# A selective scan with its decays in a ring of three buffers instead of two, the third in SBUF

## The chip, the cores and the metric

The kernel runs on one core of one Trainium2 chip. The metric is the device time of one execution in microseconds (us). The kernel before took 1248.2 us in the median of three runs (1247.94 to 1252.96). The profiler recorded one further execution.

Five engines work side by side, each through its own list of instructions: TensorE (PE; its weight loads are listed as PEld), VectorE (DVE), ScalarE (ACT), GpSimd (POOL) and SyncE (SP), which here issues the DMAs. They wait for each other by semaphores.

## The reference, cut to what matters

Four layers follow each other over 2048 tokens of 128 channels: a state-space mixer, causal attention with a mixture of eight experts, a second state-space mixer, and a gated feed-forward net. The change is in the second mixer, whose core is a linear recurrence over time, one for each of 256 channels and 16 states:

```python
delta = softplus(delta_s @ dt_proj_w + dt_proj_b)
A = -jnp.arange(1, d_state + 1)                    # d_state = 16
deltaA = jnp.exp(delta[..., None] * A)             # the decays
deltaB_u = delta[..., None] * B[:, :, None, :] * u[..., None]
def step(h, inp):
    dA, dBu_ = inp
    h = dA * h + dBu_
    return (h, h.sum(-1))                          # the sum over the 16 states
y = y + u * D
y = y * silu(z)
return y @ out_proj_w + out_proj_b
```

## The kernel before, in words

The scan stage works through NB = 4 blocks of 512 tokens, and in each through NS1 = 16 states, so 64 steps that the program numbers k = 16 b + n. The 256 channels lie as two halves (j = 0, 1) on 128 partitions. For each step:

- **ACT** writes the decays exp(-(n+1) delta) of both halves, 128 x 1024 numbers, into `decay[k % 2]` (`state_act`, L2096). The two buffers are four PSUM banks. From k = 2 on it first waits until step k - 2 has been scanned.
- **POOL** writes the drives delta u B into `drive[k % 5]` (`state_pool`, L2142), 128 x 1024 numbers. It reads `du` and a broadcast row of B, both in SBUF, and writes SBUF.
- **DVE** runs two scans of 512 tokens (`state_dve`, L2164), one for each half. Each reads its decays from PSUM and its drives from SBUF, starts from the last state of the block before (`hlast`, one number for each partition), and writes `hst[k % 4]` in SBUF.
- **PE** adds `hst` into two PSUM banks by matmuls with the identity (`state_sum_pe`, L2083), three steps behind.
- **ACT** copies the last column of `hst` into `hlast` (`state_last_act`, L2171). In its list this stands right behind the decays of step k and is for step k - 2.

DVE waits at step k for the decays and drives of k, for the sum of step k - 4 and for the copy of step k - 4, since `hst` has four buffers. POOL waits for the scan of step k - 5, since `drive` has five.

Between the steps other work is placed by tables written out by hand, each entry a step n within the block and a part: `FRONT_ACT`, `FRONT_DVE`, `FRONT_PE` and `FRONT_POOL` prepare the next block (input projection, convolution, activations, delta, u, B), `POST_*` finish the block before, `FW_ACT` and `FW_POOL` split the weights of the following net into a high and a low part (L2441 on ACT, `lo_part` L675 on POOL), and `NET_*` begin that net. On ACT the order within a step is: decays, copy of a last state, front parts, weights. Front parts that matter below are "z" and "tap" at n = 3 (L2009, L2002), "xc" and "gate" at n = 7 (L2016, L2019, in another activation table), "db" at n = 8, "dt" at n = 11 (L2040, another table again) and "u" at n = 12. On DVE "conv0" and "conv1" stand at n = 4 and 5 (L2064), "du" at n = 13 (L2075), the output of the block before (`scan_y_dve`, L2178 and L2182) ahead of step n = 3.

Before the first step the experts finish. Their last additions on DVE are L1709 (`acc`, both inputs in SBUF), their low parts on DVE are L675 (`hx_lo`, both inputs in SBUF). The low weights of the last expert lie in `ew_lo3` at offset A_END, a region of 6144 bytes of each partition that nothing uses once `down_done` is complete.

Of the kernel before, what the change touches and what calls it, by code (L numbers as in the profile page):

```python
# [5 lines left out]
F32 = mybir.dt.float32  # L6
# [3 lines left out]
ACT = mybir.ActivationFunctionType  # L10
AX = mybir.AxisListType

P = 128
T = 2048
D = 128
BLK = 512
# [16 lines left out]
NS1 = 16  # L33
HBUF = 4
DRIVE_SLOTS = 5
# [61 lines left out]
def build(nc, a):  # L97
# [10 lines left out]
    def sb(name, shape, dt, at=None):  # L108
        size = 4 if dt in (F32, F32R) else 2
        for s in shape[1:]:  # L110
            size *= s
        size = (size + 31) // 32 * 32
        if at is None:
            at = free[0]
            free[0] += size
        t = nc.alloc_sbuf_tensor_at(name, shape, dt, offset=at + BASE)
        t_end[name] = at + size
        return t

    t_end = {}  # L120
    BASE = (nc.sbuf_base + 31) // 32 * 32
    with ctx:
# [82 lines left out]
        A_END = free[0]  # L205
# [11 lines left out]
        W_END = A_END + 6144  # L217
# [100 lines left out]
        delta = sb("delta", [P, 2, 2, BLK], F32)  # L318
# [3 lines left out]
        drive = sb("drive", [P, DRIVE_SLOTS, 2, BLK], F32)  # L322
        assert t_end["drive"] - 4096 <= t_end["hid"]
        b_bc.append(sb("b_bc1", [P, B_ROWS, BLK], F32))
        hst = sb("hst", [P, HBUF, 2, BLK], F32)
# [3 lines left out]
        fh = sb("fh", [P, HC, BLK], F32)  # L329
        fo = sb("fo", [P, 2, BLK], F32)  # L330
        assert free[0] <= W_END, (free[0], W_END)
        free[0] = t_end["sz1_even"]
        fh_first = [sb("fh_hi0", [P, HC, BLK], F32R), sb("fh_lo0", [P, HC, BLK], F32R)]
        fa = sb("fa", [P, 2, BLK], F32)
# [8 lines left out]
        psum = ctx.enter_context(nc.psum_tensor("psum", [P, 8, BLK], F32))  # L343
# [791 lines left out]
        def route_at(table, k, step):  # L1135

            return table.get(LAST_STEPS * (k - 14) + step) if k >= 14 else None
# [7 lines left out]
        for k in range(16):  # L1145
            for step in range(2 * (ITEMS[k][0] + 1)):
# [8 lines left out]
                if route_at(ROUTE_PE, k, step):  # L1155
                    kind, b = route_at(ROUTE_PE, k, step)
                    plan(("route_" + kind, b))
                if (k, step) in PREP_PE:
                    b, part = PREP_PE[k, step]
# [345 lines left out]
        N_UNITS = len(UNITS)  # L1505
# [392 lines left out]
        NET_STATS, NET_LN, NET_APPLY, NET_TURN, NET_HI = 7, 9, (11, 12), 13, 14  # L1898
        b_rows = nc.dram_tensor("b_rows", (NB, NS1, BLK), F32, kind="Internal").ap()
        B_FROM = 16 * (NE // RAW_SLOTS)  # L1900
        decay = [psum[:, 4:6, :], psum[:, 2:4, :]]

        def front_parts(table, k):

            return [((k - at) // NS1 + 1, part) for at, part in table
                    if (k - at) % NS1 == 0 and 1 <= (k - at) // NS1 + 1 < NB]
# [14 lines left out]
        for k in range(NB * NS1):  # L1921
            b, n = divmod(k, NS1)
# [163 lines left out]
        def state_act(act, b, n):  # L2086
            k = NS1 * b + n
            if n == 0:
                act.wait_ge(S["c_dt_read"], 2 * b + 2)
            if k == 0:  # L2090
                act.wait_ge(S["gelu_done"], FC * N_UNITS)
            if k == 1:
                act.wait_ge(S["y_gated"], N_UNITS)
            if k >= 2:
                act.wait_ge(S["scanned"], k - 1)
            act.activation(decay[k % 2], delta[:, b % 2, :, :], ACT.Exp, scale=-float(n + 1)).then_inc(S["decay_done"], 1)  # L2096

        def b_save_sp(sp, b):
            sp.wait_ge(S["c_db_read"], b + 1)
# [55 lines left out]
        def state_dve(o, dve, b, n):  # L2155
            k = NS1 * b + n
            dve.wait_ge(S["decay_done"], k + 1)
            dve.wait_ge(S["drive_done"], k + 1)
            if k >= HBUF:
                dve.wait_ge(S["summed"], k - HBUF + 1)  # L2160
                dve.wait_ge(S["hlast_done"], k - HBUF + 1)
            for j in range(2):
                init = 0.0 if b == 0 else hlast[:, n, j:j + 1]
                ins = dve.tensor_tensor_scan(hst[:, k % HBUF, j, :], decay[k % 2][:, j, :], drive[:, k % DRIVE_SLOTS, j, :], init,  # L2164
                                             ALU.mult, ALU.add)
            ins.then_inc(S["scanned"], 1)

        def state_last_act(act, b, n):
            k = NS1 * b + n
            act.wait_ge(S["scanned"], k + 1)  # L2170
            act.activation(hlast[:, n, :], hst[:, k % HBUF, :, BLK - 1], ACT.Copy).then_inc(S["hlast_done"], 1)  # L2171
# [44 lines left out]
        def scan_act(o, act):  # L2216
            for b in range(NB):
                for n in range(NS1):
                    state_act(act, b, n)
                    if NS1 * b + n >= 2:  # L2220
                        state_last_act(act, *divmod(NS1 * b + n - 2, NS1))
                    for nb, part in front_parts(FRONT_ACT, NS1 * b + n):
                        scan_front_act(o, act, nb, part)
                    if n in FW_ACT and 3 * b + FW_ACT[n] < 11:
                        fweights_act(act, 3 * b + FW_ACT[n])
                    if b == NB - 1 and n in NET_APPLY:
                        net_apply_act(act, NET_APPLY.index(n))
                    if (b, n) == (NB - 1, NET_HI):
                        net_hi_act(act, 0)

        def scan_dve(o, dve):
            for b in range(NB):
                for n in range(NS1):
                    if n == POST_Y and b >= 1:
                        scan_y_dve(o, dve, b - 1)
                    state_dve(o, dve, b, n)
                    if b == 0 and n == 0:
                        experts_add_dve(dve, NB - 1)
                    if n == POST_DVE and b >= 1:
                        scan_post_dve(dve, b - 1)  # L2240
                    if (b, n) == (NB - 1, NET_STATS):
                        net_stats_dve(o, dve)
                    for nb, part in front_parts(FRONT_DVE, NS1 * b + n):
                        scan_front_dve(o, dve, nb, part)
            net_lo_dve(dve, 0)
            scan_y_dve(o, dve, NB - 1)
# [94 lines left out]
        def net_apply_act(act, half):  # L2341
            if half == 0:
                act.wait_ge(S["ln_rstd"], LN_D + 1)
                act.wait_ge(S["ln_turned"], LN_D)
            for i in range(TPB // 2 * half, TPB // 2 * (half + 1)):
                ins = act.activation(xn[:, i, :], x_tok[:, i, :], ACT.Identity, scale=ln_rs[:, 0, i:i + 1], bias=ln_nb[:, i:i + 1])
            if half == 1:
                ins.then_inc(S["ln_xn"], 1)

        def net_hi_act(act, b):  # L2350
            act.wait_ge(S["ln_turned"], LN_D + b + 1)
            act.activation(xT[0][:, :], net_x(b)[:, :], ACT.Copy).then_inc(S["xT_hi"], 1)
# [86 lines left out]
        def fweights_act(act, c):  # L2439
            act.wait_ge(fw_in[c % 2], 16 * (c // 2 + 1))  # L2440
            act.activation(fw_hi[:, 4 * c:4 * c + 4, :], fw_raw[:, c % 2, :, :], ACT.Copy).then_inc(S["fw_hi"], 1)  # L2441
# [95 lines left out]
        @block.scalar  # L2537
        def _(act):
            o = Order(act, S["act_order"])
            act.wait_ge(S["in_x"], 32)  # L2540
            act.activation(half_gate[:, :], cols[:, COL["b_gate"]:COL["b_gate"] + 2], ACT.Copy, scale=0.5)
            act.activation(a_neg[:, :], C("a_log"), ACT.Exp).then_inc(S["a_ready"], 1)
            for n in range(5):
                front_act(o, act, 0, n)
            for g in range(G_END):
                if g < G:
                    chunk_act(act, g)
                for what, b, n in mixer_parts(g):
                    if what == "front":
                        front_act(o, act, b, n)  # L2550
                    elif what == "prep":
                        for part in PREP_STEP_ACT[n]:
                            prep_act(act, b, part)
                    else:
                        end_act(act, b, n)
            early_act(act, "f")
            act.wait_ge(S["x_mixed"], NB)
            attention_act(act)
            moe_act(o, act)
            scan_act(o, act)  # L2560
            net_act(act)
# [173 lines left out]
```

## Time and profile before

| | |
|---|---|
| median of 3 runs | 1248.2 us |
| the profiled execution's own time | 1252.22 us |
| its span, first to last instruction | 1249.9 us |
| busy over the span | PE 90%, DVE 75%, ACT 63%, PEld 48%, POOL 26% |
| mean granted TensorE clock | 0.969 of full speed |
| scan stage | from about 910 to about 1110 us of the span |

A row of a timeline names when an instruction or a run of like instructions began, how long it took, the engine, the line of the kernel, what was written and read with shapes, how many there were, and in brackets how long the engine had been idle before it and what released it. Like instructions that follow each other are merged into one row (x2, x10). Durations of neighbours on one engine overlap by some hundredths of a us.

### The profile page before, as it was taken

Reading aid. Unit: us, or ns where it says so; the run is one execution under the profiler, and the core shown is the slowest. Engines: PE = TensorE matmul, PEld = TensorE weight load, DVE = VectorE, ACT = ScalarE, POOL = GpSimd, SP = SyncE. Lnnn points to the kernel's source line nnn. Section 1 sums busy time; section 2 is a strip of 40 time slices with the busy share of each in tenths; the row PEclk is TensorE's granted clock in tenths of the full one; section 3 lists DMA queues with packets and bytes.
Section 4 is the critical chain, followed back from the end, with each engine's and each line's share of the span. In section 5 each row is a group of like instructions: output and inputs, shape, how many; then the busy total and the mean of one; then the engine's idle time right before and its main releaser. Section 6 shows DMA issues by size and latency. Waiting matters only on the chain.

```text
span 1249.9 us, 16003 instructions
## 1 busy us (share of the span) xinstructions
PE 1120.0 (90%) x5702; PEld 594.1 (48%) x5702; DVE 931.8 (75%) x1737; ACT 783.9 (63%) x1156; POOL 327.6 (26%) x271
## 2 busy tenths in 40 slices
PE   5889878888999999989999899999979789799998
PEld 2455554443333333333322288887633334357776
DVE  4788678857887888878864188887789999984432
ACT  4767632455655656656678898667758677455554
POOL 4233332210000000000012131210179788840000
PEclk9789889999998999999999999999989999899999
DMA  5211464345000000000000132211223222200000
GB/s 152 79 41 69 122 148 102 86 102 119 2 1 1 2 1 2 1 1 1 2 19 12 42 109 66 78 51 36 84 84 111 85 110 93 102 1 6 4 9 18
DMA packets 30623, 67.29 MB, mean 54 GB/s; under 512 B 3952, under 2 KB 16240, under 8 KB 28496
## 3 DMA queue, kind: packets, MB, share of 16 engines
q1 hardware_dynamic: 30544, 66.27, 18.5%
q8 instruction: 46, 0.75, 0.3%
q14 instruction: 33, 0.27, 0.1%
HBM read 57.47 MB, written 8.78 MB: 53 GB/s over the span
## 4 chain that ended last, share of the span: by engine, by line
PE 57%; DVE 14%; POOL 9%; issue 8%; ACT 7%; DMA 1%; SPq 0%; DVEq 0%; POOLq 0%; ACTq 0%
PE psum L1353 8%; PE psum L1238 8%; PE psum L405 7%; PE psum L407 7%; PE psum L406 7%; PE psum L1307 7%; POOL drive L2142 6%; DVE mx L1250 6%; DVE hst L2164 2%; ACT probs L1321 2%; PE psum L551 1%; PE psum L543 1%; PE psum L475 1%; PE psum L1956 1%; DMA m_rows<-mrow 1%
## 5 line engine op out<-in xcount | busy, mean ns | idle before, releaser
L1250 DVE TENSOR_REDUCE mx<-psum 128x1 f32<-128x512 f32 (+3 forms) x640 | 349.2, 603 | 64.8 <-PE psum L1238 35.2
L1321 ACT ACTIVATE probs<-psum 128x1024 f32<-128x1024 f32 (+1 forms) x320 | 283.6, 936 | 173.7 <-PE psum L1307 152.7
L1238 PE MATMUL psum<-kz,qa 128*128 128x512 bf16 (+3 forms) x640 | 199.3, 354 | 18.5 <-DVE mx L1250 12.8
L1307 PE MATMUL psum<-qa,kz 128*128 128x512 bf16 (+1 forms) x640 | 176.2, 363 | 7.8 <-DMA qa<-m_rows 4.4
L2142 POOL TENSOR_TENSOR drive<-du,b_bc 128x1024 f32<-128x1024 f32 x64 | 149.5, 2367 | 10.6 <-DVE hx_lo L675 9.1
L1353 PE MATMUL psum<-probs,v 128*32 128x512 f32 (+3 forms) x1280 | 150.8, 541 | 1.5 <-POOL probs L1332 1.4
L1238 PEld LDWEIGHTS psum<-kz,qa 128*128 128x128 bf16 x640 | 57.2, 97 | 180.5 <-DVE mx L1250 131.9
L2083 PE MATMUL psum<-hst,ident 128*128 128x512 f32 x256 | 120.3, 614 | 22.7 <-DVE u L2182 14.1
L1332 POOL TENSOR_SCALAR_AFFINE_SELECT probs<-probs 128x512 f32<-128x512 f32 x48 | 29.4, 637 | 361.1 <-ACT probs L1321 361.1
L2164 DVE TENSOR_TENSOR_SCAN hst<-psum,hlast,drive 128x512 f32<-128x512 f32 x96 | 115.2, 1261 | 8.7 <-ACT psum L2096 5.0
L675 DVE TENSOR_TENSOR hx_lo<-hid,hx_hi 128x1024 fp32r<-128x1024 f32 x64 | 81.4, 1276 | 33.9 <-ACT hx_hi L1679 29.8
L2096 ACT ACTIVATE psum<-delta 128x1024 f32<-128x1024 f32 x64 | 65.6, 1026 | 51.5 <-DVE hst L2164 51.4
L1673 ACT ACTIVATE hid<-psum,cols 128x512 f32<-128x512 f32 x128 | 81.5, 681 | 21.2 <-PE psum L407 21.0
L2083 PEld LDWEIGHTS psum<-hst,ident 128*128 128x128 f32 x256 | 48.4, 196 | 88.7 <-issue 68.1
L1307 PEld LDWEIGHTS psum<-qa,kz 128*128 128x128 bf16 x640 | 57.6, 99 | 68.1 <-ACT probs L1321 27.3
L675 DVE TENSOR_TENSOR fh_lo<-fh,fh_hi 128x512 fp32r<-128x512 f32 x48 | 32.1, 688 | 57.7 <-ACT fh_hi L2371 57.7
L405 PE MATMUL psum<-fh_hi,fw_lo 128*128 128x512 f32 x144 | 57.9, 402 | 3.6 <-DVE fh_lo L675 3.6
L407 PE MATMUL psum<-fh_hi,fw_hi 128*128 128x512 f32 x144 | 56.9, 395 | 0.0
L406 PE MATMUL psum<-fh_lo,fw_hi 128*128 128x512 f32 x144 | 56.7, 394 | 0.0
L1241 PE MATMUL psum<-identb,maskneg 128*128 128x128 bf16 x256 | 55.5, 221 | 0.0
L405 PE MATMUL psum<-nx_hi,ew_lo 128*128 128x512 f32 x128 | 52.5, 411 | 3.2 <-ACT hid L1673 2.2
L2370 ACT ACTIVATE fh<-psum,cols 128x512 f32<-128x512 f32 x32 | 22.1, 689 | 48.9 <-PE psum L407 48.9
(294 smaller groups left out, 1944.6 us busy)
## 6 DMA issues: line engine op xcount, KB each, us to landing
b_bc<-b_rows SPq DMA_DIRECT2D x16, 1024.0 KB, 4.7
cs_bc<-cs_rows SPq DMA_DIRECT2D x16, 512.0 KB, 4.8
gate_bc<-gate_rows SPq DMA_DIRECT2D x32, 256.0 KB, 3.1
qk_part_rows<-qk_parts SPq DMA_DIRECT2D x48, 128.0 KB, 2.3
ew_raw<-experts_dram SPq DMA_DIRECT2D x8, 512.0 KB, 3.6
qa<-qk_part_rows SPq DMA_DIRECT2D x16, 192.0 KB, 5.3
kz<-qk_part_rows SPq DMA_DIRECT2D x16, 192.0 KB, 5.8
fw_raw<-net_dram SPq DMA_DIRECT2D x11, 256.0 KB, 2.7
```

Source lines behind the costliest of these rows:

```text
L405: pe.matmul(out, w[1], x[0], start=start, stop=False, skip_group_check=True)
L406: pe.matmul(out, w[0], x[1], start=False, stop=False, skip_group_check=True)
L407: return pe.matmul(out, w[0], x[0], start=False, stop=stop, skip_group_check=True)
L675: return dve.tensor_tensor(out, value, hi.bitcast(F32), ALU.subtract)
L1238: ins = pe.matmul(out[:, 0:w], qa[:, b, h // 2, i * P:(i + 1) * P], key_rows(h, c)[:, 0:w], start=True, stop=not last, skip_group_check=True)
L1250: dve.tensor_reduce(mx[:, 4 * i + h % 4, c:c + 1], fill_bank("mx", k, n)[:, 0:w], AX.X, ALU.max).then_inc(S["mx_read"], 1)
L1307: ins = pe.matmul(out[:, lo:], key_rows(h, kt // TPB)[:, kt % TPB * P:(kt % TPB + 1) * P], qa[:, b, h // 2, lo:], start=True, stop=not dia ...
L1321: act.activation(probs[:, st % 2, hh, :, lo:], s_pair[n % 2][:, :, lo:], ACT.Exp, scale=SCALE).then_inc(S["p_done"], 1)
L1353: ins = pe.matmul(out[32 * hh:32 * hh + 32, own:], v9[:, at:at + 32], probs[:, st % 2, hh, j, own:], start=(kt == 0), stop=(kt == TPB * (b ...
L2083: ins = pe.matmul(bank[j][:, :], ident[:, :], hst[:, (NS1 * b + n) % HBUF, j, :], start=(n == 0), stop=(n == NS1 - 1))
L2142: pool.tensor_tensor(drive[:, k % DRIVE_SLOTS, :, :], du[:, b % 2, :, :], rows.unsqueeze(1).broadcast_to([P, 2, BLK]), ALU.mult).then_inc( ...
L2164: ins = dve.tensor_tensor_scan(hst[:, k % HBUF, j, :], decay[k % 2][:, j, :], drive[:, k % DRIVE_SLOTS, j, :], init, ALU.mult, ALU.add)
```

## The change

The ring of decays gets a third buffer, `decay_sb`, 128 x 1024 floats in SBUF where `ew_lo3` lay. Step k uses buffer k % 3: steps 2, 5, 8, ... 62 (21 of 64) have their decays in SBUF, the others in PSUM as before. ACT waits for the scan of step k - 3 instead of k - 2 before it writes, and once, at k = 2, until the last expert's matmuls are done. The copy of the last state that stands behind the decays of step k is for step k - 3 instead of k - 2.

```diff
@@ -329,6 +329,8 @@
         assert free[0] <= W_END, (free[0], W_END)
+        decay_sb = sb("decay_sb", [P, 2, BLK], F32, at=A_END)
+        assert t_end["decay_sb"] <= W_END
         free[0] = t_end["sz1_even"]
@@ -1898,7 +1900,8 @@
-        decay = [psum[:, 4:6, :], psum[:, 2:4, :]]
+        decay = [psum[:, 4:6, :], psum[:, 2:4, :], decay_sb[:, :, :]]
+        ND = len(decay)
@@ -2091,9 +2094,11 @@
                 act.wait_ge(S["y_gated"], N_UNITS)
-            if k >= 2:
-                act.wait_ge(S["scanned"], k - 1)
-            act.activation(decay[k % 2], delta[:, b % 2, :, :], ACT.Exp, scale=-float(n + 1)).then_inc(S["decay_done"], 1)
+            if k == 2:
+                act.wait_ge(S["down_done"], N_UNITS)
+            if k >= ND:
+                act.wait_ge(S["scanned"], k - ND + 1)
+            act.activation(decay[k % ND], delta[:, b % 2, :, :], ACT.Exp, scale=-float(n + 1)).then_inc(S["decay_done"], 1)
@@ -2161,7 +2166,7 @@
-                ins = dve.tensor_tensor_scan(hst[:, k % HBUF, j, :], decay[k % 2][:, j, :], drive[:, k % DRIVE_SLOTS, j, :], init,
+                ins = dve.tensor_tensor_scan(hst[:, k % HBUF, j, :], decay[k % ND][:, j, :], drive[:, k % DRIVE_SLOTS, j, :], init,
@@ -2217,8 +2222,8 @@
                     state_act(act, b, n)
-                    if NS1 * b + n >= 2:
-                        state_last_act(act, *divmod(NS1 * b + n - 2, NS1))
+                    if NS1 * b + n >= ND:
+                        state_last_act(act, *divmod(NS1 * b + n - ND, NS1))
```

## Rows read from the trace of the kernel before

**Rows 1.** Scan stage: us, then busy of PE, PEld, DVE, ACT, POOL, clock, DMA share, GB/s

```profile
909.90:1109.80 199.90, 162.93 (x400) 70.77 (x398) 184.83 (x197) 128.72 (x212) 171.55 (x90) 0.95 0.26 91
```

**Rows 2.** What DVE waited for in the scan stage: total us, times, longest

```profile
DVE hst L2164 <- ACT psum L2096: 11.0, 7, 2.8
```

**Rows 3.** Timeline of DVE: scans that began late because of ACT's decays

```profile
921.18 6.89 DVE L2164 TENSOR_TENSOR_SCAN hst<-psum,drive 128x512 f32<-128x512 f32 x6 [2.76 <-ACT psum L2096]
...
954.53 4.82 DVE L2164 TENSOR_TENSOR_SCAN hst<-psum,drive 128x512 f32<-128x512 f32 x4 [1.68 <-ACT psum L2096]
...
978.13 2.46 DVE L2164 TENSOR_TENSOR_SCAN hst<-psum,hlast,drive 128x512 f32<-128x512 f32 x2 [1.10 <-ACT psum L2096]
...
1043.14 2.46 DVE L2164 TENSOR_TENSOR_SCAN hst<-psum,hlast,drive 128x512 f32<-128x512 f32 x2 [1.07 <-ACT psum L2096]
...
1054.68 4.94 DVE L2164 TENSOR_TENSOR_SCAN hst<-psum,hlast,drive 128x512 f32<-128x512 f32 x4 [1.44 <-ACT psum L2096]
```

**Rows 4.** Timeline of ACT ahead of the late scans of 954.53 and 978.13

```profile
948.42 1.03 ACT L2096 ACTIVATE psum<-delta 128x1024 f32<-128x1024 f32 x1 [1.08 <-DVE hst L2164]
...
949.60 1.28 ACT L2040 ACT_TABLE_LOAD   x1
...
974.70 1.27 ACT L2009 ACTIVATE sz_even<-psum,cols 128x512 f32<-128x512 f32 x2 [3.61 <-DVE u L2182]
```

**Rows 5.** Scan stage, groups on POOL, then DVE's scans: busy us, mean ns, idle before

```profile
L2142 POOL TENSOR_TENSOR drive<-du,b_bc 128x1024 f32<-128x1024 f32 x64 | 149.5, 2367 | 10.6 <-DVE hx_lo L675 9.1 <-issue 1.4
L675 POOL TENSOR_TENSOR fw_lo<-fw_raw,fw_hi 128x512 fp32r<-128x512 f32 x11 | 14.0, 1274 | 14.7 <-ACT fw_hi L2441 14.7
L2251 POOL TENSOR_TENSOR x_tok<-x_tok,out_b 128x512 f32<-128x512 f32 x3 | 3.8, 1267 | 6.1 <-DVE x_tok L2198 6.1
...
L2164 DVE TENSOR_TENSOR_SCAN hst<-psum,hlast,drive 128x512 f32<-128x512 f32 x96 | 115.2, 1261 | 8.7 <-ACT psum L2096 5.0 <-PE psum L2083 3.3 <-issue 0.3
```

**Rows 6.** Lines L1709 and L2142 by themselves: ns min/median/max

```profile
L1709 DVE TENSOR_TENSOR acc<-acc,y_gate x28: 661/692/2408, 745.3 to 913.5; 128x512 f32<-128x512 f32 x28
...
L2142 POOL TENSOR_TENSOR drive<-du,b_bc x64: 2338/2354/2789, 909.9 to 1104.8; 128x1024 f32<-128x1024 f32 x64
```

**Rows 7.** Timeline of POOL, then of DVE, where the drives meet DVE's last additions

```profile
909.92 2.38 POOL L2142 TENSOR_TENSOR drive<-du,b_bc 128x1024 f32<-128x1024 f32 x1 [9.15 <-DVE hx_lo L675]
...
912.26 2.79 POOL L2142 TENSOR_TENSOR drive<-du,b_bc 128x1024 f32<-128x1024 f32 x1
...
915.01 2.79 POOL L2142 TENSOR_TENSOR drive<-du,b_bc 128x1024 f32<-128x1024 f32 x1
...
910.44 2.41 DVE L1709 TENSOR_TENSOR acc<-acc,y_gate 128x512 f32<-128x512 f32 x1
...
915.52 2.32 DVE L2164 TENSOR_TENSOR_SCAN hst<-psum,drive 128x512 f32<-128x512 f32 x2
```

**Rows 8.** Timeline around 730 us, DVE and POOL by turns

```profile
730.42 1.22 DVE L675 TENSOR_TENSOR hx_lo<-hid,hx_hi 128x1024 fp32r<-128x1024 f32 x1
...
730.90 1.89 POOL L1856 TENSOR_TENSOR x_tok<-x_tok,inner 128x512 f32<-128x512 f32 x1
...
731.55 2.33 DVE L675 TENSOR_TENSOR hx_lo<-hid,hx_hi 128x1024 fp32r<-128x1024 f32 x1
...
732.75 2.27 POOL L675 TENSOR_TENSOR ew_lo<-ew_raw,ew_hi 128x512 fp32r<-128x512 f32 x1
```

**Rows 9.** Merged runs of drives and scans at the stage's end

```profile
1095.51 11.62 POOL L2142 TENSOR_TENSOR drive<-du,b_bc 128x1024 f32<-128x1024 f32 x5
...
1097.95 11.86 DVE L2164 TENSOR_TENSOR_SCAN hst<-psum,hlast,drive 128x512 f32<-128x512 f32 x10 [0.35 <-issue]
```

**Rows 10.** PE's sums at the full and at the lower clock, and the scan behind them

```profile
926.49 8.75 PE L2083 MATMUL psum<-hst,ident 128*128 128x512 f32 x20
...
1075.33 3.76 PE psum L2083 x4
...
1079.28 9.51 DVE L2164 TENSOR_TENSOR_SCAN hst<-psum,hlast,drive 128x512 f32<-128x512 f32 x8 [1.74 <-PE psum L2083]
```

## The prediction

> **What bounds the kernel now.** I read first the busy times of the stretch that the change touches [rows 1]: the scan stage lasts about 200 us, and DVE is busy for 184.8 of them, POOL for 171.6, PE for 162.9, ACT for 128.7. DVE sets the pace, and POOL is close behind. Nothing outside this stage is touched, so the change is worth what it does to these 200 us.
>
> The view of waits then says what the change could win [rows 2]: ahead of the scans DVE waited 11.0 us for decays, in 7 places. Another 3.3 us went to PE's sums, in 2 places [rows 5], and most of the rest is DVE's own work. The places stand in DVE's timeline [rows 3], where the one of 1054.68 stands for itself and one just like it at 1004.21, and the one of 978.13 also for one at 929.54.
>
> Last I read POOL, since a DVE instruction changes its kind of operands. POOL's drives take 149.5 us, its low weights 14.0 and its bias additions 3.8 [rows 5]; all of them read SBUF. Together they fill about 167 of the 200 us, so in most moments a POOL instruction that reads SBUF is running.
>
> **The change, part by part.**
>
> *Decays one step further ahead.* A third buffer helps where ACT was late because it had waited for the scan of k - 2 and then had other work to do. For each late scan of [rows 3] I asked what ACT did before:
> - 954.53, 1004.21, 1054.68 (1.68, 1.44, 1.44 us; n = 12): ACT waited for DVE, wrote the decays of n = 11 at 948.42, and only then began, at 949.60, a table load, two softplus and a second table load [rows 4], behind which the decays of n = 12 stand. With three buffers it starts that work one step (2.4 us) earlier, which covers all three. This gains up to 4.56 us.
> - 1043.14 (1.07 us; n = 8) is the same with "xc" and "gate", held by the wait for n = 7. It gains up to 1.07 us.
> - 921.18 (2.76 us): ACT stood behind the transposed input of the next block, which comes from PE. Nothing in the ring changes that.
> - 929.54 and 978.13 (1.10 us for the latter; n = 4): the decays of n = 4 stand behind "z" and "tap", which wait for PE or, at 974.70, for DVE's own output step [rows 4]. A deeper ring does not move them. No gain.
> - 1079.28, and one like it at 1028.61, wait for PE's sums, with `hst` still four deep [rows 10]. No gain.
>
> The gain is thus at most 1.68 + 1.44 + 1.44 + 1.07 = 5.6 us.
>
> *The copies of the last states.* The copy of k - 3 waits for the same scan as the decays in front of it, so it adds no wait. DVE needs the copy of k - 4 at step k; that copy now stands behind the decays of k - 1, and DVE needs the decays of k, which come later still. Nothing is queued behind a new wait. Cost 0; if this cover went, a copy of two columns a step, far less than the 1.03 us of the decays [rows 4].
>
> *The wait at k = 2* is for matmuls that must be done before the experts' last additions, which DVE ran at 910 to 915 [rows 7]; ACT comes to k = 2 after 920. Cost 0. No DMA is added or moved; the loads of B and of weights that SP issues follow the drives and splits as before.
>
> *ACT writes SBUF in 21 steps.* ACT has 71 us idle in the stage [rows 1], so a few hundredths each cost nothing.
>
> *DVE reads decays from SBUF in 21 steps, that is in 42 scans.* This is the part that decides. Today a scan reads one operand from PSUM and one from SBUF; these would read both from SBUF, and no scan in the trace does. The nearest rows are DVE additions with both inputs in SBUF. L1709 takes 661 to 692 ns, except twice, when drives ran on POOL [rows 6, 7]. The first begins at 910.44 and takes 2.41 us: POOL's drive ends at 912.30, and 0.55 us later the addition ends, so it stood until the drive was over. The next drive, at 912.26, takes 2.79 instead of 2.35 us: it stood until the addition was over. The same happens once more, at 913.55. Then the scans from 915.52 run at full speed beside the drive of 915.01, which is longer only by its wait for the addition. So a DVE instruction with two SBUF inputs and a POOL instruction that reads SBUF exclude each other, for the whole instruction, and a scan with decays in PSUM escapes that. Around 730 us one sees who is next when both have work [rows 8]: DVE, POOL (1.89 instead of 1.27 us), DVE (2.33 instead of 1.22), POOL (2.27 instead of 1.27). They take turns.
>
> The rows show this for additions, not for scans. The Trainium skill, page "SBUF — State Buffer", section "Who interferes with whom", speaks against the change in general terms: any VectorE instruction with two SBUF inputs contends with a GpSimd instruction that reads SBUF, exclusively, the loser blocked fully. By that page the sum is the one with the exclusion below; if it were true of additions alone, the sum would be the 5.6 us gained. The trace agrees for the additions (2.41 against 0.69 us).
>
> The price, from the spacing of drives and scans [rows 9]: 11.62 / 5 = about 2.31 us a drive with overlap, 11.86 / 10 = 1.19 us a scan. In an SBUF step with POOL at work, the first scan waits for the rest of a drive, on average half, 1.16 us; at its end the next drive takes its turn, and the second scan waits for all of it, 2.31 us. That is 3.47 us. The 21 steps cost 21 x 3.47 = 73 us if POOL always has such an instruction. It has about 167 us of them in a stage of 200 + x us, where x is what the stage grows by: 73 x 167 / (200 + x) - 5.6 = x gives x = 44. That is +44 us.
>
> Bounds: below, the shared path alone must carry 64 x 2.31 + 11 x 1.22 + 3 x 1.22 (POOL) + 42 x 1.19 (scans) = 215 us, where POOL's stretch is now 197 us (909.9 to 1107.1, [rows 7, 9]): +18 us. Above, POOL never idle and still 5.6 gained: +67 us. I take 44, since POOL's waits for ACT and DVE (14.7 + 6.1 + 1.4 = 22 us now, [rows 5]) stay in the program. That a scan from SBUF is itself shorter or longer is bounded by a few hundredths of a us in 42 scans, about 1 us either way: taken as 0.
>
> The profiled execution itself took 1252.2 us, so by the sum 1252.2 + 44 = 1296; it stands 4 us above the median of the runs. Against the median the same sum gives 1248.2 + 44 = **1292 us**.
>
> **The rivals.**
> 1. *No exclusion for scans; the gain alone* (the other side). The scan's second operand might be fetched otherwise than an addition's. Then all of 5.6 us is kept if POOL keeps up; a drive ended at 1095.51 + 2.31 = 1097.82, and its scan began at 1097.95 [rows 9], so POOL is close and some may be lost. Time 1242.6 to 1248. It decides this way if drives beside SBUF scans stay at 2.35 us. Against it: the exclusion shows in every row where both had two SBUF inputs.
> 2. *Exclusion, but both scans of a step in one turn.* DVE queues its second scan before the first ends; if POOL doesn't get in between, DVE waits only for the rest of one drive, and POOL is held for 2 x 1.19 us in 21 steps. Then the shared path's sum rules: +18 us with POOL never idle, +18 + 22 with its idle kept; the middle is +29, or 1277 us. Against it: [rows 8], where POOL got its turn between two DVE instructions.
> 3. *Exclusion and a slower TensorE.* PE's four matmuls of a step took 3.76 us after idle time, where 8.75 / 5 = 1.75 is usual [rows 10]. With steps of 3.8 us and longer holes, PE idles more, and the clock (0.95 in this stage, [rows 1]) can fall to 1.2 GHz more often, each time with a wait like the 1.74 us there. Eight such falls: +13 us, 1305 us.
> 4. *The change does nothing:* the ring is never used beyond two, 1248 us. The late scans of n = 12 speak against it.
>
> **How the numbers follow.** The sum above (turns): 0.70, 1292 us, itself 1275 to 1308. Rival 3: 0.10. Rival 2: 0.08. Rival 1: 0.10. Rival 4: 0.02. The range from 1266 to 1316 holds the first three, 0.88 less the tails of the sum, about 0.8. About 0.5% (6.2 us) is what a measurement can tell from no change. Faster by more needs the whole gain and a little more: 0.03. Within 0.5%: the rest of rivals 1 and 4, 0.08. Slower: 0.89.
>
> **What would show it.** In the changed profile the scans split into those from `psum` and those from `decay_sb`; the first stay at 1.26 us [rows 5], the 42 others should average over 2 us, with some near 3.5. Drives should have a maximum near 3.5 us and a mean near 2.8. DVE's waits for the decays should fall from 11.0 to about 5.4 us, the places at n = 12 gone. The scan stage should be some 44 us longer and all else the same. If the scans from `decay_sb` stay at 1.26 us, rival 1 is right; if only the first of each pair is long, rival 2; if DVE waits mostly for L2083, rival 3.

## The result and the profile after

The changed kernel takes 1291.3 us in the median of four runs (1288.1 to 1294.0), the kernel before 1248.1 us in its runs beside them. The ratio is 1.034, with a 95% interval of 1.032 to 1.037: 43 us slower. The forecast was 1292 us, within 1266 to 1316. Single executions far above all others of their kernel (2184 and 1427 us among the experiments) are left out of every time below.

The profiled execution took 1291.3 us, its span is 1288.9 us. Its scan stage, from the first scan of `hst` to the end of the last, lasts from 909.2 to 1148.6, that is 239.5 us; before it was 915.5 to 1109.8, 194.3 us. These are 45 us more. What follows the stage takes 140 us in both. The stage begins at different times in different executions of the same kernel (909.2 and 914.4 us in two of the changed one, whose stages last 239.5 and 239.4 us), so profiles are compared by the stage and not by their span. All of the loss lies where the change is.

The row of [rows 1] begins 5.6 us ahead of the first scan. Here is the stage from the first scan on, of the kernel before and then of the changed one (us, then busy us and number of instructions of PE, PEld, DVE, ACT and POOL, then clock, DMA share and GB/s):

```profile
915.50:1109.80 194.30, 161.19 (x392) 69.70 (x392) 179.30 (x194) 127.05 (x210) 165.97 (x88) 0.95 0.25 89
...
909.10:1148.70 239.60, 173.15 (x392) 74.96 (x393) 225.42 (x194) 127.22 (x209) 194.70 (x88) 0.86 0.20 72
```

DVE is busy for 225 instead of 179 us with the same 194 instructions. They take longer. The groups of scans and of drives (busy us, mean ns, idle before) show which, and answer to [rows 5]:

```profile
L2169 DVE TENSOR_TENSOR_SCAN hst<-psum,hlast,drive 128x512 f32<-128x512 f32 x64 | 77.3, 1256 | 4.3 <-PE psum L2086 3.5 <-issue 0.9
L2169 DVE TENSOR_TENSOR_SCAN hst<-decay_sb,hlast,drive 128x512 f32<-128x512 f32 x32 | 75.1, 2386 | 2.9 <-PE psum L2086 1.5 <-ACT psum L2101 1.1 <-issue 0.3
L2169 DVE TENSOR_TENSOR_SCAN hst<-psum,drive 128x512 f32<-128x512 f32 x22 | 25.3, 1198 | 4.7 <-ACT psum L2101 4.7
L2169 DVE TENSOR_TENSOR_SCAN hst<-decay_sb,drive 128x512 f32<-128x512 f32 x10 | 22.0, 2239 | 0.0
...
L2147 POOL TENSOR_TENSOR drive<-du,b_bc 128x1024 f32<-128x1024 f32 x64 | 171.5, 2708 | 11.4 <-DVE hx_lo L677 9.1 <-DVE hst L2169 1.2 <-issue 1.1
```

Scans with decays in PSUM take what they took, 1.26 and 1.20 us. The 42 with decays in `decay_sb` took longer by 32 x (2.386 - 1.256) + 10 x (2.239 - 1.198) = **46.6 us**. The drives on POOL grew from 2.37 to 2.71 us in the mean. One step shows how. These are timeline rows of DVE and POOL, put next to each other:

```profile
996.40 2.34 POOL L2147 TENSOR_TENSOR drive<-du,b_bc 128x1024 f32<-128x1024 f32 x1
...
996.99 2.82 DVE L2169 TENSOR_TENSOR_SCAN hst<-decay_sb,hlast,drive 128x512 f32<-128x512 f32 x1
...
998.70 3.26 POOL L2147 TENSOR_TENSOR drive<-du,b_bc 128x1024 f32<-128x1024 f32 x1
...
999.74 3.30 DVE L2169 TENSOR_TENSOR_SCAN hst<-decay_sb,hlast,drive 128x512 f32<-128x512 f32 x1
```

The first scan starts in the middle of a drive, stands until the drive ends at 998.74, and runs. Meanwhile the next drive stands (3.26 us), gets its turn when the scan ends at 999.81, and now the second scan stands through it, until 1003.04. One step's two scans took 6.05 us in place of 2.5.

The waits of DVE in the stage (total us, times, longest) answer to [rows 2]:

```profile
DVE hst L2169 <- ACT psum L2101: 5.8, 4, 2.8
DVE hst L2169 <- PE psum L2086: 5.0, 3, 1.7
DVE x_tok L2203 <- PE psum L2196: 2.2, 1, 2.2
DVE hst L2169 <- issue: 1.2, 2, 0.9
```

The view puts 5.8 us down to ACT where it was 11.0 before, 5.0 + 2.2 us to PE where it was 3.3, and 1.2 us to nothing visible where it was 0.3. Waits in sum: 14.6 before, 14.2 after. With the 46.6 us of longer scans this makes 46 us, and the stage grew by 45.2.

The releasers need a second look, since this view puts no wait of a scan down to POOL's drives. Rows of POOL, ACT and DVE for step 59 (n = 11 of the last block):

```profile
1130.29 2.35 POOL L2147 TENSOR_TENSOR drive<-du,b_bc 128x1024 f32<-128x1024 f32 x1
...
1125.39 1.06 ACT L2101 ACTIVATE decay_sb<-delta 128x1024 f32<-128x1024 f32 x1 [2.37 <-DVE hst L2169]
...
1132.73 3.30 DVE L2169 TENSOR_TENSOR_SCAN hst<-decay_sb,hlast,drive 128x512 f32<-128x512 f32 x1 [1.07 <-ACT psum L2101]
```

The decays of this step were ready at 1126.45, its drive only at 1132.64, and the scan began 0.09 us later. So this wait of 1.07 us was for POOL, and so were the two under "issue" (0.27 and 0.89 us), whose scans too began 0.09 us behind the end of their drive. Sorted anew, waits for ACT fell by 6.3 us (11.0 to 4.7), those for PE rose by 3.9 and those for POOL by 1.9 (0.3 to 2.2).

### The profile page after: what moved, and what is told of

Its sections match the earlier page's. It is cut to its first block and busy times, and to the rows that moved or that the text cites. A ratio compares the mean times of both kernels' runs of the same rounds, so it can differ in the third digit from the quotient of the medians.

```text
span 1288.9 us, 16002 instructions
## 1 busy us (share of the span) xinstructions
PE 1126.9 (87%) x5702; PEld 596.1 (46%) x5702; DVE 978.8 (76%) x1737; ACT 783.5 (61%) x1155; POOL 356.0 (28%) x271
## 5 line engine op out<-in xcount | busy, mean ns | idle before, releaser
L2086 PE MATMUL psum<-hst,ident 128*128 128x512 f32 x256 | 132.6, 663 | 62.4 <-DVE hst L2169 33.4
L2147 POOL TENSOR_TENSOR drive<-du,b_bc 128x1024 f32<-128x1024 f32 x64 | 171.5, 2708 | 11.4 <-DVE hx_lo L677 9.1
L2086 PEld LDWEIGHTS psum<-hst,ident 128*128 128x128 f32 x256 | 51.2, 209 | 137.3 <-issue 83.7
L2169 DVE TENSOR_TENSOR_SCAN hst<-psum,hlast,drive 128x512 f32<-128x512 f32 x64 | 77.3, 1256 | 4.3 <-PE psum L2086 3.5
L2169 DVE TENSOR_TENSOR_SCAN hst<-decay_sb,hlast,drive 128x512 f32<-128x512 f32 x32 | 75.1, 2386 | 2.9 <-PE psum L2086 1.5
L2101 ACT ACTIVATE psum<-delta 128x1024 f32<-128x1024 f32 x43 | 44.0, 1023 | 26.0 <-DVE hst L2169 25.9
```

The lines of the kernel that those rows point to most:

```text
L2086: ins = pe.matmul(bank[j][:, :], ident[:, :], hst[:, (NS1 * b + n) % HBUF, j, :], start=(n == 0), stop=(n == NS1 - 1))
L2147: pool.tensor_tensor(drive[:, k % DRIVE_SLOTS, :, :], du[:, b % 2, :, :], rows.unsqueeze(1).broadcast_to([P, 2, BLK]), ALU.mult).then_inc( ...
```

## The experiments

Eight different kernels and two repeats. Stage means first scan to last scan's end in the profiled execution: 194.3 us before, 239.5 us after.

### The third buffer in PSUM: is the depth good by itself?

```diff
-        decay = [psum[:, 4:6, :], psum[:, 2:4, :], decay_sb[:, :, :]]
+        third = None
+        decay = [psum[:, 4:6, :], psum[:, 2:4, :], third]
...
+            if k % ND == 2:
+                act.activation(bank[1], delta[:, b % 2, 1, :], ACT.Exp, scale=-float(n + 1)).then_inc(S["decay_done"], 1)
+                return
...
-                ins = pe.matmul(bank[j][:, :], ident[:, :], hst[:, (NS1 * b + n) % HBUF, j, :], start=(n == 0), stop=(n == NS1 - 1))
+                ins = pe.matmul(bank[0][:, :], ident[:, :], hst[:, (NS1 * b + n) % HBUF, j, :],
+                                start=(n == 0 and j == 0), stop=(n == NS1 - 1 and j == 1))
...
```

Both scans of such a step read `bank[1]`, and DVE's output step reads the sums of `bank[0]` for both halves.

> The ring stays three deep, but the third buffer is one PSUM bank instead of SBUF: it holds the decays of the second half only, and both scans of steps 2, 5, ... 62 read it; to free that bank, PE adds both halves' states into one bank. Left out: the first half's own decays in those 21 steps, and separate sums of the two halves; ACT's write in those steps is 512 instead of 1024 wide. Theory (a scan with two SBUF inputs and a POOL instruction that reads SBUF exclude each other; depth itself helps): 1242.6 us, 5.6 below the kernel before, DVE's waits for decays down from 11.0 to about 5.4 us, all scans at 1.25 us, all drives at 2.35 us. Rival (the deeper ring or the moved copy costs something by itself): 1250 us or more with all scans short.

Measured: 1244.7 us, ratio 0.997 (0.995 to 1.000); the stage lasts 190.6 us, 3.7 less than before. Its groups of scans, its drives, and DVE's waits:

```profile
L2174 DVE TENSOR_TENSOR_SCAN hst<-psum,hlast,drive 128x512 f32<-128x512 f32 x96 | 114.9, 1262 | 7.1 <-PE psum L2087 4.8 <-issue 1.2 <-ACT psum L2106 1.1
...
L2152 POOL TENSOR_TENSOR drive<-du,b_bc 128x1024 f32<-128x1024 f32 x64 | 149.6, 2371 | 9.4 <-DVE hx_lo L677 9.1 <-issue 0.3
...
DVE hst L2174 <- ACT psum L2106: 5.8, 4, 2.8
DVE hst L2174 <- PE psum L2087: 4.8, 3, 1.7
DVE hst L2174 <- issue: 1.2, 2, 0.8
```

All scans and drives have their old length, and the waits for ACT fell to 5.8 us. Depth is not the culprit. It is worth less than forecast: of 5.2 us won from ACT, 1.5 went to waits for PE's sums and 0.9 to waits without a visible releaser, where DVE began 0.09 us behind the end of the step's drive on POOL. PE adds three steps behind and `hst` has four buffers, so a DVE that comes earlier to n = 4 waits there for PE (1.34 us at n = 4 of the second block, where it waited 1.10 us for ACT before).

### The SBUF buffer without the depth

```diff
-            if k >= ND:
-                act.wait_ge(S["scanned"], k - ND + 1)
+            if k >= 2:
+                act.wait_ge(S["scanned"], k - 1)
...
-                    if NS1 * b + n >= ND:
-                        state_last_act(act, *divmod(NS1 * b + n - ND, NS1))
+                    if NS1 * b + n >= 2:
+                        state_last_act(act, *divmod(NS1 * b + n - 2, NS1))
```

> Three buffers, the third in SBUF as in the change, but the decays of step k wait for the scan of k - 2 and the copy behind them is for k - 2, as before. Exclusion: the gain of depth is gone and the price stays, 1291 plus at most 5.6: 1291 to 1297 us; scans from decay_sb average about 2.4 us. Rival (the loss comes from the depth or from the moved copies): 1248 us.

Measured: 1295.1 us, ratio 1.039 (1.035 to 1.042). The loss is all there without the depth and without the moved copies; the rival is out. The stage lasts 238.4 us, no longer than with the depth, and the intervals of the two ratios overlap: beside the slow scans the depth brings nothing that can be told. DVE waited 7.4 us for ACT here, against 5.8 by the same view with the depth.

### POOL writes but doesn't read

```diff
-            pool.tensor_tensor(drive[:, k % DRIVE_SLOTS, :, :], du[:, b % 2, :, :], rows.unsqueeze(1).broadcast_to([P, 2, BLK]),
-                               ALU.mult).then_inc(S["drive_done"], 1)
+            o.did(pool.memset(out[:, 0, :], 0.01))
+            o.wait()
+            o.did(pool.memset(out[:, :, :], 0.01))
+            o.wait()
+            pool.memset(out[:, :, :], 0.01).then_inc(S["drive_done"], 1)
```

> The changed kernel, with each drive on POOL replaced by three memsets of the same tile (512, 1024 and 1024 wide), which read nothing: the products delta u B are left out. Exclusion against POOL's reads: scans from decay_sb at 1.25 us but for those beside the 11 weight splits and the bias additions, DVE's time ahead of the kernel before; 1243 us if a step's memsets take no longer than 2.35 us together, up to 1256 if they take 2.5. Rival (a scan whose decays lie in SBUF is slow whatever POOL does): scans from decay_sb still 2.4 us on average, 1285 to 1291 us. Rival (POOL's writes exclude as well): as slow as the changed kernel, or slower.

Measured: 1248.5 us, ratio 1.000 (0.998 to 1.002). The groups of the scans from SBUF and of one of the memsets, then the scans from SBUF by ns min/median/max:

```profile
L2172 DVE TENSOR_TENSOR_SCAN hst<-decay_sb,hlast,drive 128x512 f32<-128x512 f32 x32 | 41.4, 1334 | 4.8 <-ACT psum L2101 2.5 <-PE psum L2086 1.9 <-ACT decay_sb L2101 0.3
L2172 DVE TENSOR_TENSOR_SCAN hst<-decay_sb,drive 128x512 f32<-128x512 f32 x10 | 13.0, 1340 | 0.0
...
L2149 POOL MEMSET drive<- 128x1024 f32 x64 | 60.9, 952 | 3.7
...
L2172 DVE TENSOR_TENSOR_SCAN hst<-decay_sb,hlast,drive x32: 1249/1260/2236, 963.0 to 1106.0; 128x512 f32<-128x512 f32 x32
L2172 DVE TENSOR_TENSOR_SCAN hst<-decay_sb,drive x10: 1192/1200/1959, 919.2 to 957.3; 128x512 f32<-128x512 f32 x10
```

This is the sharpest of the runs. The same scans read the same SBUF buffer, POOL is about as busy as before (60.9 + 60.9 + 33.7 us of memsets for 149.5 us of drives), and 37 of the 42 scans take 1.19 to 1.29 us. The other five take 1.60 to 2.24 us, and each of them began while one of POOL's weight splits or bias additions ran, which do read SBUF and remain in this kernel. They cost 4 us, and the stage lasts 198.5 us, 4.2 more than before. So a scan whose decays lie in SBUF is not slow in itself, and POOL's memsets, which only write, don't hold it up. The instructions on POOL that read two SBUF operands do; whether one that reads a single one would was not run.

### One scan instead of two in the SBUF steps

```diff
+            if k % ND == 2:
+                init = 0.0 if b == 0 else hlast[:, n, 0:1]
+                both = "p j t -> p (j t)"
+                ins = dve.tensor_tensor_scan(hst[:, k % HBUF, :, :].rearrange(both), decay[2].rearrange(both),
+                                             drive[:, k % DRIVE_SLOTS, :, :].rearrange(both), init, ALU.mult, ALU.add)
+                ins.then_inc(S["scanned"], 1)
+                return
```

> The changed kernel, with one scan over 1024 columns instead of two over 512 in the 21 steps whose decays lie in SBUF: the second half's own initial state is left out. Taking turns: POOL no longer gets in between the halves, so DVE waits only for the rest of one drive, at most 2.3 and on average 1.2 us in a step; 1267 to 1280 us, about 20 below the changed kernel. Rival (each such scan is slow by a fixed share, 2.39 for 1.25 us): the long scan takes about 4.6 us and the time stays at 1291 us.

Measured: 1272.2 us, ratio 1.020 (1.017 to 1.023), 19 us below the change; the stage lasts 218.8 us. The long scans:

```profile
L2170 DVE TENSOR_TENSOR_SCAN hst<-decay_sb,hlast,drive 128x1024 f32<-128x1024 f32 x16 | 59.6, 3728 | 4.0 <-ACT psum L2101 2.1 <-PE psum L2086 1.9
L2170 DVE TENSOR_TENSOR_SCAN hst<-decay_sb,drive 128x1024 f32<-128x1024 f32 x5 | 15.0, 2999 | 0.0
```

The shortest took 2.26 and 2.32 us in the two groups, so the 21 waited 59.6 + 15.0 - 21 x 2.3 = 26 us, 1.25 us a step, about half a drive, as the rule of turns says. The columns and bytes are the same as in the change, only the number of turns is halved. A fixed slowdown would not have changed. One thing stays open: the first scans of the change waited 0.86 us on average, and why a long scan waits more, 1.25 us, no run shows.

### The change again, shorter drives, and more steps in SBUF

> The changed kernel once more, unchanged, on the same chip as the runs beside it: 1291 us, 1.034 of the kernel before. It is the measure for the next two.

Measured: 1292.7 us, ratio 1.034 (1.030 to 1.039). Its 42 scans from SBUF were busy for 97.1 us, as in the first profile, and its stage lasts 239.4 us.

Next, shorter drives in the changed kernel (called e6 in the expectations):

```diff
-            pool.tensor_tensor(drive[:, k % DRIVE_SLOTS, :, :], du[:, b % 2, :, :], rows.unsqueeze(1).broadcast_to([P, 2, BLK]),
-                               ALU.mult).then_inc(S["drive_done"], 1)
+            for j in range(2):
+                ins = pool.tensor_tensor(drive[:, k % DRIVE_SLOTS, j, :], du[:, b % 2, j, :], rows, ALU.mult)
+            ins.then_inc(S["drive_done"], 1)
```

> The changed kernel with each drive on POOL as two instructions of 512 columns instead of one of 1024; nothing is left out. Taking turns for whole instructions: the rest of a drive that the first scan waits for is 0.6 us on average instead of 1.16, and the one that gets in between is 1.2 instead of 2.31 us, so the price halves, but POOL has about 0.13 us more to do in each of 64 steps and carries 223 us of reads in the stage: 1270 to 1280 us. Scans from decay_sb at most 2.5 us long (3.3 in the changed kernel). Rival (an SBUF scan is slowed by a fixed share whenever POOL is busy): 1291 us or more, scans from decay_sb as long as before.

Measured: 1285.0 us, ratio 1.029 (1.026 to 1.033). This is outside the expected 1270 to 1280, and its interval overlaps that of the change (1.030 to 1.039), so the times alone hardly show a gain. The scans do: all but two of the 42 were at most 2.37 us long, most of the second ones 2.22, where the change has 3.30, so the wait goes by the length of POOL's instruction. These 40 scans waited 30 us in all, against 47 us of all 42 in the change. The two others stood far longer and waited 14 us, which the forecast did not have. Timeline rows of POOL and of DVE around the first:

```profile
1049.94 6.16 POOL L2148 TENSOR_TENSOR drive<-du,b_bc 128x512 f32<-128x512 f32 x5
...
1049.94 7.23 DVE L2170 TENSOR_TENSOR_SCAN hst<-decay_sb,hlast,drive 128x512 f32<-128x512 f32 x1
```

Five instructions of POOL ran one after the other while the scan stood, until POOL had nothing left that it could start. The other took 9.12 us. The profiled execution was the slowest of the four (1291.1 us). I ran the same kernel again for its profile:

> The kernel of e6 once more, for its profile. There two scans from decay_sb stood 7.2 and 9.1 us, through five and more drives of POOL in a row, where all others waited for one drive at most. If a turn is sometimes missed by the moment at which the scan asks, the long waits recur, at the same or at other places, and account for 10 us or more of the stage. If they were a disturbance of that one execution, no scan is longer than 2.5 us and the stage is 12 us shorter than in e6.

One execution, 1281.5 us. The first long wait did not come back, the second did, at the same step (k = 53), 9.14 us long. Its rows:

```profile
1096.64 1.30 POOL L677 TENSOR_TENSOR fw_lo<-fw_raw,fw_hi 128x512 fp32r<-128x512 f32 x1
1097.90 7.36 POOL L2148 TENSOR_TENSOR drive<-du,b_bc 128x512 f32<-128x512 f32 x6
...
1097.21 9.14 DVE L2170 TENSOR_TENSOR_SCAN hst<-decay_sb,hlast,drive 128x512 f32<-128x512 f32 x1
```

This scan asked in the middle of a POOL instruction and not at the seam of two, so the moment of asking alone, as I had put it, does not explain a missed turn. What does stays open. The stage lasted 237.3 us in the first execution and 231.2 in this one; the difference of 6.1 us is the one long wait less (7.23 - 1.25 = 6.0).

In the kernel before, with its ring of two, the short drives cost nothing:

> The kernel before (decays in PSUM) with each drive in two instructions of 512 columns. No exclusion is left but with the experts' last additions; POOL has 64 x 0.13 = 8 us more to do in a stage where it idles 22 us: 1248 to 1256 us, all scans at 1.25 us. That is the part of e6 that has nothing to do with the third buffer.

Measured: 1245.7 us, ratio 0.998 (0.996 to 1.000), stage 194.7 us. That is 2 us below the expected range: POOL's longer work cost nothing that can be told. The 3 us that it may have won are not in the stage and too near to the interval's end for a claim. DVE's additions at L1709 that [rows 6] show at up to 2.41 us are at most 1.46 us long here.

With every second step in SBUF:

```diff
-        decay = [psum[:, 4:6, :], psum[:, 2:4, :], decay_sb[:, :, :]]
+        decay = [psum[:, 4:6, :], decay_sb[:, :, :]]
...
-            if k == 2:
+            if k == 1:
                 act.wait_ge(S["down_done"], N_UNITS)
```

> A ring of two, banks 4 and 5 of PSUM and the SBUF buffer, so that every second step (32 of 64) has its decays in SBUF; the wait is for the scan of k - 2 as before. Exclusion with turns: 32 x 3.47 = 111 us if POOL always reads, and 111 x 167 / (200 + x) = x gives x = 70: 1318 us. By the price per step measured in the changed kernel (2.2 us) 32 steps cost 70 us as well. If POOL becomes the bound, its reads and 64 scans take 241 us against 197 now: at least +44, 1292 us. Rival (only the first few steps or certain places of the schedule pay): below 1300 us.

Measured: 1312.8 us, ratio 1.051 (1.047 to 1.055). The groups of its SBUF scans:

```profile
L2169 DVE TENSOR_TENSOR_SCAN hst<-decay_sb,hlast,drive 128x512 f32<-128x512 f32 x48 | 113.4, 2402 | 0.0
...
L2169 DVE TENSOR_TENSOR_SCAN hst<-decay_sb,drive 128x512 f32<-128x512 f32 x16 | 33.0, 2102 | 3.0 <-ACT decay_sb L2101 3.0
```

64 scans took longer by 48 x (2.402 - 1.256) + 16 x (2.102 - 1.198) = 69 us in 32 steps, 2.2 us a step, as in the change (46.6 / 21 = 2.2). The price goes by the number of such steps, not by places of the schedule. The stage grew by only 61 us (255.1), since DVE's waits fell to about 7 us.

### A cure for other late scans, with the ring of two

```diff
-        FRONT_ACT = [(-1, "apply"), (0, "hi"), (2, "x"), (3, "z"), (3, "tap"), (7, "xc"), (7, "gate"), (8, "db"), (11, "dt"), (12, "u")]
+        FRONT_ACT = [(-1, "apply"), (0, "hi"), (2, "x"), (4, "z"), (4, "tap"), (7, "xc"), (7, "gate"), (8, "db"), (11, "dt"), (12, "u")]
```

> The kernel before (ring of two in PSUM) with one edit: ACT does the parts z and tap of the next block behind the decays of n = 4 instead of n = 3, so that these decays no longer wait for DVE's output step. The late scans of 929.54 (1.47 us) and 978.13 (1.10 us) go; those at n = 4 of the later blocks wait for PE and stay: 1 to 2.6 us less, 1246 to 1247 us. Rival (what is gained there is lost as a later convolution or a later weight split on POOL): no change, 1248 us.

Measured: 1247.7 us, ratio 1.000 (0.998 to 1.002). No change: the rival's time, but not by its cause. DVE's waits:

```profile
DVE hst L2164 <- ACT psum L2096: 8.4, 5, 2.8
DVE hst L2164 <- PE psum L2083: 5.1, 4, 1.7
```

2.6 us of waits for ACT are gone, and 1.8 us came back as waits for PE: the two steps that had waited 1.47 and 1.10 us for ACT now waited 0.56 and 1.48 us for PE. This is the same give-back as with the third buffer in PSUM. No version of mine is clearly faster than the kernel before. The third buffer in PSUM (0.995 to 1.000), which leaves out part of the work, and the short drives (0.996 to 1.000) come nearest.

## Why the prediction was right

**The price of the SBUF scans** decided, as forecast. The sum had 44 + 5.6 = 50 us for it, the trace shows 46.6. Per step it put 3.47 x 167 / 244 = 2.4 us, measured are 2.2. Instruction by instruction, first scans waited 0.86 us on average (forecast 1.16 x 0.68 = 0.8), second scans 1.37 (2.31 x 0.68 = 1.6). Of the 21 second scans 13 stood through a whole drive, two through a shorter instruction, six through none. A whole drive cost 3.30 - 1.25 = 2.05 and not 2.31 us: the wait is a little shorter than the spacing of drives by which I had priced it. That is the small error of this term. POOL's drives took 2.71 us in the mean and 3.28 at most, where the forecast had about 2.8 and 3.5.

One of the rows behind it was misread: L1709 does not take "661 to 692 ns, except twice", since 692 is its median. Three more of its 28 additions were long, 1.24, 1.01 and 1.45 us at 784.68, 790.73 and 812.28. At each of these times POOL ran its splits of L675, which read SBUF, so these additions bear the exclusion out too.

The Trainium skill (page "SBUF — State Buffer", section "Who interferes with whom") speaks of any VectorE instruction with two SBUF inputs, and the prediction took this to hold for scans. The runs agree: 2.39 us in the mean beside POOL's reads, 1.19 to 1.29 us beside its memsets alone, 1.26 us with the decays in PSUM. The same section of the Trainium skill says that a GpSimd instruction that only writes does not contend; the run with memsets agrees.

**The gain of the deeper ring** was put at 5.6 us, and this term was wrong in its parts. Two rows of the changed kernel's DVE:

```profile
957.17 2.34 DVE L2169 TENSOR_TENSOR_SCAN hst<-psum,drive 128x512 f32<-128x512 f32 x2 [1.40 <-ACT psum L2101]
...
984.99 3.43 DVE L2169 TENSOR_TENSOR_SCAN hst<-decay_sb,hlast,drive 128x512 f32<-128x512 f32 x2 [1.55 <-PE psum L2086]
```

The late scans at n = 12 and at 1043.14 went, as forecast. But in the first block DVE waited for ACT one step later, at n = 13, behind ACT's "u" part. The wait of 929.54, said to stay, shrank from 1.47 to 0.53 us. The one of 978.13 (n = 4 of the second block), also said to stay, became a wait of 1.55 us for PE: the working asked what DVE waited for, and not what it would wait for next. POOL's drives came late in three places. So ACT's share fell by 5.2 us (6.3 with the wait at 1132.73 put down to POOL), near the forecast 5.6 partly by luck, and waits for PE and POOL took nearly all of it back. With PSUM buffers 3.7 us of the stage remained; with the SBUF buffer next to nothing (14.6 against 14.2 us of waits). The two errors, about 4 us too much price and 5 us too much gain, cancel, so 1292 is nearer to 1291.3 than the working deserved.

**Costs set to zero** were zero where they could be read: the copies and the wait at k = 2 appear in no wait of DVE.

**The rivals.** No exclusion for scans: out by the groups of the first profile. Both scans in one turn: out by the rows at 996 us; the kernel with one scan shows what that would have been, 1272 us, where I had 1277. A slower TensorE: the granted clock in the stage fell from 0.95 to 0.86, with PE's matmuls no more than before in a longer stage, and DVE's waits for PE rose by 3.9 us, not by 13. How much of the 3.9 the clock made is not shown; 1.5 us of it also came with the third buffer in PSUM, where no scan was long and the clock was 0.93. A ring that does nothing: out, as ACT's waits fell.

## What to carry to other kernels

Before moving an operand of a VectorE instruction from PSUM to SBUF, look whether its other operand is in SBUF as well and whether GpSimd reads SBUF at that time. If so, each such instruction waits for the GpSimd instruction in progress and lets the next one in behind it: here 2.2 us for each pair of scans of 1.25 us, 46.6 us in all, to win 5 to 6 us of waits for ACT. If it can't be avoided, fewer and longer VectorE instructions lower the price (19 us of 43 here). Shorter GpSimd ones shorten the single wait (2.05 to 0.97 us), but only 7 us of the time went with them, which is hardly clear of noise. And read, for every wait that goes, what the engine would wait for next: of the lateness of ACT that two of the runs removed, 5.2 and 2.6 us, waits for PE took back 1.5 and 1.8 us. Where the view of waits names no releaser, look when the other inputs of the instruction were ready: here it was a drive of POOL.

## What was not expected of the hardware

The turns are not kept always. With drives of 512 columns, a scan with two SBUF inputs stood 7.23 us and another 9.12 us while five or more POOL instructions ran in a row, and ended only when POOL had no instruction to start. The same kernel had one such wait of 9.14 us in a second execution. With drives of 1024 columns no scan of the change was longer than 3.35 us in either profile. Which condition lets POOL keep the read path was not found.
